# Attention's pipeline step -2 moves beside the patch stage, and the weights' transfers are issued in pieces

## The chip, the core and the metric

The kernel runs on one core of one Trainium2 chip. The metric is the time of one launch in microseconds (us), the median of several runs. The core has five engines with an instruction stream each: PE multiplies matrices, DVE and POOL work elementwise on the on-chip memory (SBUF), ACT does scaled copies and exponentials, and SP only issues transfers (DMAs). They meet through semaphores.

## The reference

64 images of 3 x 224 x 224 become 64 x 196 tokens of 192 numbers; two attention layers, an MLP and a mixture of four experts follow.

```python
x = patches of 16 x 16 x 3                           # one row of 768 for each of 64 * 196 tokens
x = layernorm(x, ln1_g, ln1_b) @ W + b
h = layernorm(x, ln2_g, ln2_b)                       # "tokens", 12544 x 192
h = h + attention(layernorm(h))                      # 12 heads of 16, over the 196 tokens of an image
n = layernorm(h)
x = n + attention(layernorm(n, g, b)); x = x + mlp(x)
h = h + x + (the two best of 4 experts(layernorm(x)), weighted)
```

## The kernel before

`vit_tower` (L2333 and after) runs two blocks. In the first, `attention_phase` builds the programs of the two attention layers and calls `tokenize_phase`, the patch stage; in the second, `ffn_phase` does the MLP and the experts. Names of tiles begin with `t_` in the patch stage, with `a_` in attention and with `f_` after it.

*The patch stage.* The images are read in 8 groups of 16 images and 7 rows of patches, into two row buffers (`rows`) that take turns. A group has 7 units of two patch columns each, so there are 56 units. `steps` (in `tokenize_phase`) is written out for s = -3 to 56, and in each step every engine does its part of up to four units, by `LAG`: "A" is unit s+3 (DVE: statistics of the rows), "B" is unit s+1 (ACT normalises to `xn`, PE turns it, ACT and DVE split it into a high half `xh` and a low half `xl`), "C" is unit s (PE: the product with the weights into `yp`, DVE: its statistics), "D" is unit s-1 (ACT: L1356 writes `t_yn`; POOL: L1292 and L1294 apply gain and offset; SP: L1263 stores it to `tokens`). POOL works out scale and shift for "A" and "C" in four small instructions (L1305 to L1311). There are four `t_yn` buffers, and ACT waits for the store of unit u-4 before it writes unit u. SP loads the next group's rows (L1234) in four quarters, in the steps of a group's first four units.

*What runs beside it.* After each of its steps every engine calls its own `beside_patches(s)` of attention, a list written by hand: which part of attention's preparation it does after step s. There the weights of both layers are loaded (`load_weights`, SP, after steps 4 and 5), turned by PE, scaled by ACT and split by DVE, and the first units of layer 0 are started.

*Attention.* A unit is two images, 392 tokens; a layer has 32 units, so there are 64. A unit goes through a pipeline: load ("W", 5 steps ahead), scale and norm on POOL ("X", 4 ahead), turning, high and low halves and two row products ("L", 3 ahead), the third row product, the stores to a scratch tensor `a_qk` and the first half of its stacks `qst` and `kst` ("P", 2 ahead), the other half, row maxima and values ("M", 1 ahead), scores, exponentials and weighted sums ("C"), and three steps behind that. `steps` (in `attention_phase`) runs s = -2 to 66, partly in loops. Step -2 holds "W" of unit 3, "X" of unit 2, "L" of unit 1 and "P" of unit 0; step -1 has the first maxima, step 0 the first exponentials. Each engine starts its part (`attend`) when it is through with the patch stage, after waits: PE for all of the patch stage's `t_yn` and for 12 settings (`set_s`), of which the six memsets of `stack_borders` on DVE are the last.

*Memory.* `qst`, `kst`, `vp` and `pt` are allocated after the patch stage's tiles are released, so they lie where these lay and can't be written before the patch stage is over.

## Time and profile before

| what | value |
|---|---|
| median of 3 runs | 3089.83 us (3086.55 to 3103.68) |
| the profiled execution | 3087.19 us |
| its span | 3085.5 us |
| PE, DVE, ACT, POOL busy | 89%, 75%, 61%, 55% |
| patch stage and weights | 0 to about 371 us |
| attention steps -2 and -1 | about 371 to 404 us |
| attention, two layers | about 405 to 1850 us |
| experts | about 1850 us to the end |

The profile is one execution, read on the core's own clock from 0. A row of a timeline says when an engine ran an instruction (or some of one kind after each other, "x2"), how long, and in brackets how long the engine had been idle before it and who released it. The granted clock is TensorE's: 1.00 is its full 2.4 GHz, 0.50 the lower level of 1.2 GHz, and what lies between is a stretch with both.

### The profile page before, as it was taken

The numbers are of one execution on the slowest core, as the hardware profiler recorded it, in microseconds if no ns is written. First come the engines' busy times: TensorE is split into PE (matmuls) and PEld (weight loads), VectorE is DVE, ScalarE is ACT, GpSimd is POOL, SyncE is SP. The second block draws the span as 40 slices with busy tenths as digits, with TensorE's granted clock in tenths as the row PEclk, the third lists the DMA queues.
The fourth block names the chain that finished last, engine by engine and source line by source line (L and its number), as shares of the span: only waits on it lengthen the run. The fifth ranks groups of instructions, "written<-read, shape, count | busy, mean of one in ns | idle before, by whom it ended". The sixth has DMA issues, their size and how long they took to land. (4 is left out here: it accounts for less than half of the span.)

```text
span 3085.5 us, 95504 instructions
## 1 busy us (share of the span) xinstructions
PE 2732.0 (89%) x31491; PEld 2124.6 (69%) x31491; DVE 2311.9 (75%) x5326; ACT 1878.1 (61%) x3798; POOL 1682.0 (55%) x1957
## 2 busy tenths in 40 slices
PE   5798788999899998989998967999986999999998
PEld 5688645555555555555555546899975888888887
DVE  5689678788878887877788735877765777777776
ACT  5577556667666666666666636777753444444443
POOL 3467635555455666667666432567674444444444
PEclk9899989999999999999999968999987999999999
DMA  6555256676766667676767635444433444444443
GB/s 159 161 157 166 58 121 155 145 164 149 157 142 152 165 163 167 161 173 160 175 159 174 143 76 136 147 147 147 143 126 91 68 67 65 68 67 65 69 66 47
DMA packets 515433, 395.07 MB, mean 128 GB/s; under 512 B 223136, under 2 KB 488386, under 8 KB 515138
## 3 DMA queue, kind: packets, MB, share of 16 engines
q1 hardware_dynamic: 431426, 310.47, 41.3%
q0 software_dynamic: 38496, 46.38, 8.5%
q10 hardware_dynamic: 45216, 34.34, 4.6%
q8 instruction: 179, 2.93, 0.4%
q14 instruction: 116, 0.95, 0.1%
HBM read 232.59 MB, written 155.42 MB: 126 GB/s over the span
## 5 line engine op out<-in xcount | busy, mean ns | idle before, releaser
L814 DVE TENSOR_REDUCE a_mx<-a_mxp 98x4 f32<-98x784 f32 x768 | 747.0, 973 | 268.6 <-PE a_mxp L1000 265.9
L603 ACT ACTIVATE a_pt<-a_st 98x784 f32<-98x784 f32 x768 | 634.6, 826 | 352.8 <-PE a_st L986 351.9
L1817 POOL DMA_INDIRECT out_dram<-f_yo,f_idg x202 | 330.9, 1638 | 415.6 <-DVE f_yo L2158 378.9
L500 POOL TENSOR_TENSOR a_cf<-a_ctxs,a_rec 128x1176 f32<-128x1176 f32 x64 | 171.6, 2681 | 448.1 <-DMA a_rec<-a_recip 448.1
L1895 ACT ACTIVATE f_hf<-f_bank,f_b1c 128x256 f32<-128x256 f32 x606 | 254.3, 473 | 236.0 <-PE f_bank L1128 236.0
L1015 PE MATMUL a_pv<-a_pt,a_vp 98*32 98x196 f32 x6144 | 358.7, 352 | 5.0 <-issue 4.1
L986 PE MATMUL a_st<-a_qst,a_kst 49*128 49x196 f16 x3072 | 266.7, 253 | 78.6 <-DMA a_qst<-a_mrow 53.5
L2320 PE MATMUL f_bank<-f_w2h,f_hh 128*128 x1212 | 298.9, 247 | 19.0 <-DVE f_hl L2142 18.7
L2321 PE MATMUL f_bank<-f_w2h,f_hl 128*128 x1212 | 298.2, 246 | 0.0
L2322 PE MATMUL f_bank<-f_w2l,f_hh 128*128 x1212 | 298.2, 246 | 0.0
L1000 PE MATMUL a_mxp<-a_kst,a_qst 48*128 48x196 f16 x3072 | 263.6, 250 | 28.8 <-DVE a_mx L814 21.5
L986 PEld LDWEIGHTS a_st<-a_qst,a_kst 49*128 49x128 f16 x3072 | 88.2, 95 | 280.2 <-ACT a_pt L603 131.0
L1015 PEld LDWEIGHTS a_pv<-a_pt,a_vp 98*32 98x32 f32 x6144 | 215.8, 151 | 72.9 <-issue 58.6
L1788 POOL DMA_INDIRECT f_listed<-f_xr,f_idx x196 | 209.6, 1069 | 76.1 <-issue 44.5
L1128 PE MATMUL f_bank<-f_el,f_w1h 128*128 128x256 f16 x1212 | 232.1, 273 | 0.0
L2142 DVE TENSOR_TENSOR f_hl<-f_hf,f_hh 128x512 f16<-128x512 f32 x303 | 209.9, 693 | 10.4
L1848 ACT ACTIVATE f_hh<-f_bank,f_b1c 128x256 f16<-128x256 f32 x294 | 141.0, 480 | 107.9 <-PE f_bank L1128 105.5
L1887 ACT ACTIVATE f_xf<-f_bank,f_bcol,f_gcol 128x256 f32<-128x256 f32 x202 | 103.2, 561 | 169.1 <-PE f_bank L2290 169.1
L1000 PEld LDWEIGHTS a_mxp<-a_kst,a_qst 48*128 48x128 f16 x3072 | 123.2, 96 | 78.8 <-DVE a_mx L814 62.7
L1128 PE MATMUL f_bank<-f_eh,f_w1h 128*128 128x256 f16 x606 | 165.6, 273 | 3.5 <-DVE f_el L2132 3.5
L1128 PE MATMUL t_yp<-t_wh,t_xh 128*112 128x192 f16 x672 | 168.2, 250 | 0.0
L1128 PE MATMUL t_yp<-t_wl,t_xh 128*112 128x192 f16 x672 | 167.6, 249 | 0.0
(314 smaller groups left out, 8269.9 us busy)
## 6 DMA issues: line engine op xcount, KB each, us to landing
a_rec<-a_recip SPq DMA_DIRECT2D x256, 147.0 KB, 4.9
t_rows<-in_x_dram SPq DMA_DIRECT2D x84, 392.0 KB, 5.7
a_qst<-a_qk SPq DMA_DIRECT2D x256, 110.2 KB, 3.2
a_kst<-a_qk SPq DMA_DIRECT2D x256, 110.2 KB, 4.0
f_xg<-f_listed SPq DMA_DIRECT2D x101, 264.0 KB, 2.8
a_qk<-a_qkh SPq DMA_DIRECT2D x128, 196.0 KB, 3.1
a_qk<-a_qkl SPq DMA_DIRECT2D x128, 98.0 KB, 3.4
a_qk<-a_qkh SPq DMA_DIRECT2D x128, 98.0 KB, 2.5
```

The lines of the kernel that those rows point to most:

```text
L603: act.activation(pt[k % PT][:].rearrange("p j a t -> p j (a t)"), st_ps[0:half_t, :, 0:unit_t], ACT.Exp, scale=sm_scale).then_inc(exp_s, 1)
L814: dve.tensor_reduce(mx[:, a, :, 2 * p:2 * p + 2].rearrange("p q j -> p j q"), mx_ps[0:half_t, :, 0:unit_t].rearrange("p j (q t) -> p j q t ...
L986: ins = pe.matmul(st_ps[:, j, kt * tok:(kt + 1) * tok], kst[b][part, p, a, at:at + 128], qst[b][part, p, a, 0:tok], start=True, stop=True)
L1000: ins = pe.matmul(mx_ps[:, j, qt * tok:(qt + 1) * tok], qst[b][part, p, a, at:at + 128], kst[b][part, p, a, 0:tok], start=True, stop=True)
L1015: ins = pe.matmul(pv_ps[32 * h4:32 * h4 + 32, 0:tok], vp[b][:, 2 * a + kt, :].rearrange("p (c h) -> p c h", h=heads)[:, :, h], pt[(first + ...
L1128: ins = pe.matmul(out, lhs, rhs, start=(i == 0), stop=(i == len(terms) - 1))
L1817: pool.indirect_dma_start(out, bass.IndirectOffsetOnAxis(ap=idg[i % 3][:, t:t + 1], axis=0), yo[i % 3][:, t, :], None, compute_op=ALU.add) ...
L1895: act.activation(hf[pair][:, c % 2, :], p1[q % 2][:, (c % 2) * T:(c % 2) * T + T], ACT.Gelu, bias=b1c[:, bass.ds(e, 1), c], scale=1.0 / WS ...
L2142: dve.tensor_tensor(hl[i % 2][:, cs, :], hf[pair][:], hh[i % 2][:, cs, :], ALU.subtract).then_inc(ehl_s, 1)
L2320: pe.matmul(o, hh[i % 2][:, j, ts], high, start=(j == 0), stop=False)
L2321: pe.matmul(o, hl[i % 2][:, j, ts], high, start=False, stop=False)
L2322: pe.matmul(o, hh[i % 2][:, j, ts], low, start=False, stop=False)
```

## The change

`load_weights` is cut into four functions with the same transfers, which SP issues after other steps of the patch stage: layer 0's after steps 3, 4 and 5, layer 1's after steps 10, 11, 12 and 17. The work of attention's step -2 goes into the `beside_patches` lists of all five engines, and what stood in these lists for the first units is put some steps earlier. `steps` of attention begins at -1. So that stacks can be filled while patches are worked on, `qst`, `kst`, `vp` and half of the `pt` buffers are allocated before everything else, and the first row buffer, `rows0`, is laid over them: it is read for the last time by the seventh group, the last but one. The memsets of `kst` move from DVE to POOL (after steps 50 and 55) with a semaphore of their own, `edge_s`, for which SP and PE wait; the wait for the last `t_yn` moves from PE's `attend` into the first `turn_maxima`. The lists of the diff are, in order, SP's, POOL's, ACT's, DVE's and PE's.

```diff
+        shared = -(-nc.sbuf_base // 32) * 32
+        qst = [sb(f"qst{i}", [128, pairs, 2, tok + PAD], F16) for i in range(2)]
+        kst = [sb(f"kst{i}", [128, pairs, 2, tok + PAD], F16) for i in range(2)]
+        vp = [sb(f"vp{i}", [half_t, 4, 32 * heads], F32) for i in range(2)]
+        pt = [sb(f"pt{i}", [half_t, 2, 2, tok], F32) for i in range(PT // 2)]
+        assert nc.sbuf_base - shared >= 4 * 3 * 16 * 224
...
-            at = -2
+            at = -1
...
-            def load_weights(layer):
+            def load_input_weights(layer):
...
+            def load_input_biases(layer):
...
+            def load_output_weights(layer):
...
+            def load_vectors(layer):
...
             def beside_patches(s):
+                if s == 3:
+                    load_input_weights(0)
+                    load_input_biases(0)
                 if s == 4:
-                    load_weights(0)
+                    load_output_weights(0)
                 if s == 5:
-                    load_weights(1)
-                if s == 38:
+                    load_vectors(0)
+                if s == 10:
+                    load_input_weights(1)
+                if s == 11:
+                    load_input_biases(1)
+                if s == 12:
+                    load_output_weights(1)
+                if s == 17:
+                    load_vectors(1)
+                if s == 34:
                     for done in patches["stored"]:
                         sp.wait_ge(done, 16 * 4)
                     load_rows(0, 0, 0)
-                if s == 41:
+                if s == 37:
                     load_rows(1, 1, 0)
-                if s == 48:
+                if s == 46:
                     load_rows(2, 0, 0)
+                if s == 51:
+                    store_parts(0, 0, 0)
+                    store_parts(0, 0, 1)
+                    store_parts(0, 0, 2)
+                if s == 52:
+                    store_parts(0, 0, 3)
+                if s == 53:
+                    sp.wait_ge(edge_s, 1)
+                    load_stacks(0, 0, 0, 0)
+                    load_stacks(0, 0, 0, 1)
+                if s == 54:
+                    load_rows(3, 1, 0)
...
-                sp.wait_ge(set_s, SET)
+                sp.wait_ge(edge_s, 2)
...
-                if s == 42:
+                if s == 39:
                     scale_tokens(0, 0, 0)
-                if s == 43:
+                if s == 40:
                     norm_tokens(0, 0, 0)
+                if s == 46:
+                    scale_tokens(1, 1, 0)
                 if s == 47:
-                    scale_tokens(1, 1, 0)
-                if s == 48:
                     norm_tokens(1, 1, 0)
+                if s == 50:
+                    pool.wait_ge(patches["read"], patches["reads"])
+                    pool.memset(kst[0][:], MROW).then_inc(edge_s, 1)
+                if s == 53:
+                    scale_tokens(2, 0, 0)
+                if s == 54:
+                    norm_tokens(2, 0, 0)
+                if s == 55:
+                    pool.memset(kst[1][:], MROW).then_inc(edge_s, 1)
...
-                if s == 45:
+                if s == 42:
                     high_part(0, 0, 0)
                     high_part(0, 0, 1)
+                if s == 46:
+                    high_rows(0, 0, 0, 0)
+                if s == 47:
+                    high_rows(0, 0, 1, 0)
                 if s == 49:
-                    high_rows(0, 0, 0, 0)
-                if s == 50:
-                    high_rows(0, 0, 1, 0)
+                    high_rows(0, 0, 2, 0)
+                if s == 52:
+                    high_part(1, 1, 0)
+                    high_part(1, 1, 1)
+                if s == 55:
+                    high_rows(1, 1, 0, 0)
+                if s == 56:
+                    high_rows(1, 1, 1, 0)
...
-            def stack_borders():
+            def borders(i):
                 dve.wait_ge(patches["read"], patches["reads"])
-                for i in range(2):
-                    dve.memset(kst[i][:], MROW).then_inc(set_s, 1)
-                    dve.memset(qst[i][:, :, :, tok:tok + PAD], 0.0).then_inc(set_s, 1)
-                    dve.memset(vp[i][:, :, 2 * dim - heads:2 * dim], 1.0).then_inc(set_s, 1)
+                dve.memset(qst[i][:, :, :, tok:tok + PAD], 0.0).then_inc(set_s, 1)
+                dve.memset(vp[i][:, :, 2 * dim - heads:2 * dim], 1.0).then_inc(set_s, 1)
...
-                if s == 40:
+                if s == 36:
                     statistics(0, 0, 0)
+                if s == 37:
                     statistics(0, 0, 2)
+                if s == 38:
+                    aggregate(0, 0)
                 if s == 41:
-                    aggregate(0, 0)
+                    statistics(1, 1, 0)
+                if s == 42:
+                    statistics(1, 1, 2)
+                if s == 43:
+                    low_part(0, 0, 0)
                 if s == 44:
-                    statistics(1, 1, 0)
+                    low_part(0, 0, 1)
                 if s == 45:
-                    low_part(0, 0, 0)
-                if s == 46:
-                    low_part(0, 0, 1)
-                    statistics(1, 1, 2)
                     aggregate(1, 0)
+                if s == 47:
+                    low_rows(0, 0, 0, 0)
+                if s == 48:
+                    low_rows(0, 0, 1, 0)
+                if s == 49:
+                    statistics(2, 0, 0)
                 if s == 50:
-                    low_rows(0, 0, 0, 0)
+                    low_rows(0, 0, 2, 0)
                 if s == 51:
-                    low_rows(0, 0, 1, 0)
+                    statistics(2, 0, 2)
                 if s == 52:
-                    statistics(2, 0, 0)
+                    aggregate(2, 0)
+                    borders(0)
+                if s == 53:
+                    low_part(1, 1, 0)
+                    low_part(1, 1, 1)
+                if s == 54:
+                    borders(1)
+                if s == 55:
+                    statistics(3, 1, 0)
+                if s == 56:
+                    low_rows(1, 1, 0, 0)
+                    low_rows(1, 1, 1, 0)
...
-                stack_borders()
...
-                if s == 44:
+                if s == 41:
                     pe.wait_ge(w_f[1], G_READY[1] + 4)
                     turn_rows(misc[BANK["T0"]], 0, 0)
                     turn_rows(misc[BANK["T1"]], 0, 1)
-                if s == 48:
+                if s == 45:
                     for layer in range(NL):
                         pe.wait_ge(w_ok[layer], 5)
-                    rows(take("QK0", -3), 0, 0, 0, 0)
-                if s == 49:
-                    rows(take("QK1", -3), 0, 0, 1, 0)
+                    pe.wait_ge(xl_s, 1)
+                    rows(misc[BANK["QK0"]], 0, 0, 0, 0)
+                if s == 46:
+                    pe.wait_ge(xl_s, 2)
+                    rows(misc[BANK["QK1"]], 0, 0, 1, 0)
+                if s == 48:
+                    pe.wait_ge(ql_s, 1)
+                    rows(misc[BANK["QK2"]], 0, 0, 2, 0)
+                if s == 51:
+                    pe.wait_ge(ql_s, 3)
+                    turn_rows(misc[BANK["T0"]], 1, 0)
+                    turn_rows(misc[BANK["T1"]], 1, 1)
+                if s == 54:
+                    pe.wait_ge(xl_s, 3)
+                    rows(misc[BANK["QK0"]], 1, 1, 0, 0)
+                if s == 55:
+                    pe.wait_ge(xl_s, 4)
+                    rows(misc[BANK["QK1"]], 1, 1, 1, 0)
...
+                if isinstance(u, int) and u == 0 and a == 0:
+                    pe.wait_ge(patches["normed"], patches["norms"])
...
-                pe.wait_ge(patches["normed"], patches["norms"])
                 pe.wait_ge(set_s, SET)
+                pe.wait_ge(edge_s, 2)
...
-        qst = [sb(f"qst{i}", [128, pairs, 2, tok + PAD], F16) for i in range(2)]
-        kst = [sb(f"kst{i}", [128, pairs, 2, tok + PAD], F16) for i in range(2)]
-        vp = [sb(f"vp{i}", [half_t, 4, 32 * heads], F32) for i in range(2)]
-
-        pt = [sb(f"pt{i}", [half_t, 2, 2, tok], F32) for i in range(PT)]
+        pt += [sb(f"pt{i}", [half_t, 2, 2, tok], F32) for i in range(PT // 2, PT)]
...
-        rows = [sb(f"rows{i}", [R, chans, line], F32) for i in range(2)]
+        rows = [nc.alloc_sbuf_tensor_at("t_rows0", [R, chans, line], F32, offset=told["rows0"]), sb("rows1", [R, chans, line], F32)]
...
-        told["read"], told["reads"] = xn_s, 2 * NU
+        told["read"], told["reads"] = xn_s, 2 * ((n_groups - 1) * UPG)
```

The first place is SP's queue around the weights (each row issues transfers; `t_rows` are image rows, which a `_50` behind the name doesn't change; `tokens<-t_yn` is a store of the patch stage). Before, the end of layer 1's 31 transfers, ahead of the third group's rows and a store:

```order
L289 DMA a_praw<-in_L_ffn_out_w_dram 96x12x16
L292 DMA a_pbias<-in_L_ffn_out_b_dram 96x1 x2
L295 DMA a_bv<-in_L_ffn_in_b_dram 98x192
L299 DMA a_gcol<-in_L_ffn_ln_g_dram 128x1
L301 DMA a_gcol<-in_L_ffn_ln_g_dram 64x1 x2
L299 DMA a_bcol<-in_L_ffn_ln_b_dram 128x1
L301 DMA a_bcol<-in_L_ffn_ln_b_dram 64x1 x2
L1234 DMA t_rows<-in_x_dram 112x1x896 [waits t_st_s,t_xn_s]
L1234 DMA t_rows<-in_x_dram 112x1x896 x2
L1263 DMA tokens<-t_yn 16x7x384 [waits t_aff]
L1234 DMA t_rows<-in_x_dram 112x1x896 x3
```

Now, at the same rows of the third group:

```order
L314 DMA a_bv<-in_L_attn_b_qkv_dram 98x192
L1324 DMA t_rows_50<-in_x_dram 112x1x896 [waits t_st_s,t_xn_s]
L1324 DMA t_rows_50<-in_x_dram 112x1x896 x2
L1353 DMA tokens<-t_yn 16x7x384 [waits t_aff]
L1324 DMA t_rows_50<-in_x_dram 112x1x896 x3
L1353 DMA tokens<-t_yn 16x7x384 [waits t_aff]
L1324 DMA t_rows_50<-in_x_dram 112x1x896 x3
L1353 DMA tokens<-t_yn 16x7x384 [waits t_aff]
L1324 DMA t_rows_50<-in_x_dram 112x1x896 x3
L1353 DMA tokens<-t_yn 16x7x384 [waits t_aff] x2
L272 DMA a_wraw<-in_L_ffn_in_w_dram 96x1x192
```

Layer 1's transfers stand behind the group's rows now, and stores stand between their four pieces.

The second place is POOL's stream at the end of the patch stage in the new kernel (numbers are buffer numbers; `t_shift1` ends the part of step 55, `t_yn3` is the last unit):

```order
L1395 TENSOR_TENSOR t_rstd1<-t_mv1,t_eps 112x2 [waits t_yn_s,t_mv2_s]
L1397 TENSOR_TENSOR t_rstd1<-t_rstd1,t_minus_half 112x2 [waits t_norm_s]
L1399 TENSOR_TENSOR t_shift1<-t_mv1,t_rstd1 112x2 [waits t_norm_s]
L1401 TENSOR_TENSOR t_shift1<-t_shift1,t_minus_one 112x2 [waits t_norm_s]
L498 MEMSET a_kst1 128x2712
L1382 TENSOR_TENSOR t_yn3<-t_yn3,t_g2 112x384 [waits t_yn_s]
L1384 TENSOR_TENSOR t_yn3<-t_yn3,t_b2 112x384 [waits t_aff]
L1199 UNCONDITIONAL_BRANCH
```

The memset is new here; before, `t_yn3` followed `t_shift1` at once.

The third place is PE's stream where the patch stage ends (the branch) and attention begins. Before:

```order
L1128 MATMUL t_yp1<-t_brow_parts,t_first_two 112x192
L1121 UNCONDITIONAL_BRANCH
L1045 MATMUL a_misc0<-a_ident,a_xn 128x98 [waits a_ql_s,a_xn_s,a_set_s,t_yn_s]
L1045 MATMUL a_misc0<-a_ident,a_xn 128x98 x3
L1047 MATMUL a_misc1<-a_ident,a_xn 128x98 [waits a_xn_s,a_ql_s]
L1047 MATMUL a_misc1<-a_ident,a_xn 128x98 x3
L1128 MATMUL a_misc0<-a_xh0,a_wh0 128x392 [waits a_xl_s]
```

Now:

```order
L1218 MATMUL t_yp1<-t_brow_parts,t_first_two 112x192
L1218 MATMUL a_misc1<-a_xh1,a_wh0 128x392 [waits a_xl_s]
L1218 MATMUL a_misc1<-a_xh1,a_wl0 128x392
L1218 MATMUL a_misc1<-a_xl1,a_wh0 128x392 x2
L1218 MATMUL a_misc1<-a_xl1,a_wl0 128x392
L1211 UNCONDITIONAL_BRANCH
L1218 MATMUL a_misc0<-a_wh0,a_xh0 128x192 [waits a_ql_s,a_edge_s,a_set_s]
```

The turned rows (`a_ident`) and the row products (128x392) stand ahead of the branch now, and attention begins with a value product (128x192), which waits for `a_edge_s` and no longer for `t_yn_s`.

## Rows read from the trace of the kernel before

**Rows 1.** The page: busy time of each engine (share of the span) x instructions.
```profile
PE 2732.0 (89%) x31491; PEld 2124.6 (69%) x31491; DVE 2311.9 (75%) x5326; ACT 1878.1 (61%) x3798; POOL 1682.0 (55%) x1957
```

**Rows 2.** Stretches: start:end, length, busy time of engines, granted clock, DMA share, GB/s.
```profile
80.00:92.00 12.00, 11.21 (x121) 10.40 (x122) 11.11 (x40) 9.60 (x14) 8.75 (x16) 1.00 0.26 43
...
92.00:104.00 12.00, 2.64 (x32) 2.46 (x30) 2.74 (x11) 0.63 (x2) 0.28 (x2) 0.69 0.63 168
```

**Rows 3.** Timeline of ACT: start us, duration, engine, line, instruction, [idle before <-releaser].
```profile
87.41 0.91 ACT L1356 ACTIVATE t_yn<-t_yp,t_shift,t_rstd 112x192 f32<-112x192 f32 x2 [0.56 <-POOL t_shift L1311]
...
103.37 0.91 ACT L1356 ACTIVATE t_yn<-t_yp,t_shift,t_rstd 112x192 f32<-112x192 f32 x2 [11.62 <-DMA tokens<-t_yn]
...
124.12 0.91 ACT L1356 ACTIVATE t_yn<-t_yp,t_shift,t_rstd 112x192 f32<-112x192 f32 x2 [0.43 <-POOL t_shift L1311]
```

**Rows 4.** Timeline of SP's queue (each row is the issuing of DMAs).
```profile
74.63 0.59 SPq L1263 DMA_DIRECT2D tokens<-t_yn  x1
...
75.26 0.77 SPq L264 DMA_DIRECT2D a_wraw<-in_L_ffn_in_w_dram  x1
...
94.72 1.10 SPq L301 DMA_DIRECT2D a_bcol<-in_L_ffn_ln_b_dram  x2
...
95.95 1.92 SPq L1234 DMA_DIRECT2D t_rows<-in_x_dram  x3
...
97.91 0.62 SPq L1263 DMA_DIRECT2D tokens<-t_yn  x1
...
104.29 1.88 SPq L1234 DMA_DIRECT2D t_rows<-in_x_dram  x3
```

**Rows 5.** Timeline of DVE, the wait for the third group of image rows.
```profile
117.24 1.94 DVE L1389 BATCH_NORM_STATS2 t_stats<-t_rows 112x6 f32<-112x384 f32 x4 [22.05 <-DMA t_rows<-in_x_dram]
```

**Rows 6.** Timeline of ACT and of POOL: one undisturbed patch step.
```profile
280.29 0.91 ACT L1356 ACTIVATE t_yn<-t_yp,t_shift,t_rstd 112x192 f32<-112x192 f32 x2 [0.57 <-POOL t_shift L1311]
...
285.27 0.91 ACT L1356 ACTIVATE t_yn<-t_yp,t_shift,t_rstd 112x192 f32<-112x192 f32 x2 [0.63 <-POOL t_shift L1311]
...
281.28 1.00 POOL L1292 TENSOR_TENSOR t_yn<-t_yn,t_g 112x384 f32<-112x384 f32 x1 [1.03 <-ACT t_yn L1356]
...
285.04 0.20 POOL L1311 TENSOR_TENSOR t_shift<-t_shift,t_minus_one 112x4 f32<-112x4 f32 x1
```

**Rows 7.** Timeline of ACT around scale_tokens(0) and norm_tokens(0) on POOL.
```profile
295.89 0.91 ACT L1356 ACTIVATE t_yn<-t_yp,t_shift,t_rstd 112x192 f32<-112x192 f32 x2 [0.59 <-POOL t_shift L1311]
...
301.54 0.91 ACT L1356 ACTIVATE t_yn<-t_yp,t_shift,t_rstd 112x192 f32<-112x192 f32 x2 [1.29 <-POOL t_shift L1311]
...
308.30 0.91 ACT L1356 ACTIVATE t_yn<-t_yp,t_shift,t_rstd 112x192 f32<-112x192 f32 x2 [1.33 <-POOL t_shift L1311]
```

**Rows 8.** Timeline of DVE: one attention instruction beside the patches.
```profile
338.99 0.59 DVE L844 SCALAR_TENSOR_TENSOR a_qkl<-a_misc,a_bq,a_qkh 128x392 f16<-128x392 f32 x1
```

**Rows 9.** Timeline of POOL and DVE: memsets, and POOL's last patch row.
```profile
51.94 0.56 POOL L415 MEMSET a_pbias<- 96x256 f32 x2
...
366.89 0.20 POOL L1311 TENSOR_TENSOR t_shift<-t_shift,t_minus_one 112x2 f32<-112x2 f32 x1
...
364.57 2.32 DVE L683 MEMSET a_kst<- 128x2712 f16 x1 [0.51 <-issue]
```

**Rows 10.** The end of the patches: a stretch, and PE's timeline.
```profile
362.00:371.00 9.00, 1.68 (x18) 1.51 (x15) 6.50 (x13) 1.83 (x4) 5.62 (x10) 0.74 0.13 39
...
370.32 0.88 PE L1045 MATMUL a_misc<-a_ident,a_xn 98*128 98x98 f32 x4 [7.32 <-issue]
...
380.15 0.26 PE L1128 MATMUL a_misc<-a_wh,a_xh 128*128 128x192 f16 x1 [0.57 <-DVE a_qkl L844]
...
384.64 0.34 PE L1000 MATMUL a_mxp<-a_kst,a_qst 48*128 48x196 f16 x4 [2.67 <-DMA a_kst<-a_qk]
```

**Rows 11.** DVE's first maximum; the tile view of `a_pt`: durations, first and last start.
```profile
385.02 0.98 DVE L814 TENSOR_REDUCE a_mx<-a_mxp 98x4 f32<-98x784 f32 x1 [4.16 <-PE a_mxp L1000]
...
L603 ACT ACTIVATE a_pt<-a_st x768: 808/824/864, 404.7 to 1822.8; 98x784 f32<-98x784 f32 x192
```

More of the change, by code:

```diff
@@ L151, in attention_phase @@
         set_s = sem("set_s")
+        edge_s = sem("edge_s")
         p_ok = [sem(f"p_ok{i}") for i in range(NL)]
@@ L245, in attention_phase @@
         g_rows, r_rows, o_rows = [[layer[i].rearrange("(t p) d -> p t d", p=half_t) for layer in layers] for i in range(3)]
-        W_READY, G_READY, W_LOADS, SET = [], [], [], 12
+        W_READY, G_READY, W_LOADS, SET = [], [], [], 10
         for *_, head_major, affine in layers:
@@ L267, in load_weights @@
                     sp.dma_start(wraw[layer][:, 4:6, dim:256], w_rows[:, 4:6, 128:dim]).then_inc(w_in[layer], 16)
+                else:
+                    sp.dma_start(wraw[layer][:, :, 0:dim], w_rows).then_inc(w_in[layer], 16)
+                    sp.dma_start(wraw[layer][:, :, dim:256], w_rows[:, :, 128:dim]).then_inc(w_in[layer], 16)
+            def load_input_biases(layer):
+                _, _, _, w_qkv, b_qkv, w_proj, b_proj, head_major, affine = layers[layer]
+                if head_major:
                     b_rows = b_qkv[0:2 * dim].rearrange("(w h d) -> w d h", w=2, h=heads)
@@ L293, in load_weights @@
                                      b_proj[e * rows_q:(e + 1) * rows_q].rearrange("(p o) -> p o", o=1)).then_inc(w_in[layer], 16)
+            def load_vectors(layer):
+                _, _, _, w_qkv, b_qkv, w_proj, b_proj, head_major, affine = layers[layer]
                 bv_row = b_qkv[2 * dim:3 * dim]
@@ L1069, in attend @@
             def attend():
-                pe.wait_ge(patches["normed"], patches["norms"])
                 pe.wait_ge(set_s, SET)
+                pe.wait_ge(edge_s, 2)
                 steps(step, pe)
             return beside_patches, attend
-        patches = {}
+        patches = {"rows0": shared}
         sync_early, sync_attend = sync_program(nc.sync, patches)
```

3 lines of the change are left out of this document (1 added, 2 removed).

## Prediction

> **What bounds the kernel now.** I read the page, then the busy time by stretches, then the timelines of each engine over the first 410 us. The reader is to see two things. First, no engine limits the whole: PE is busy 89% of the span and DVE 75% [rows 1], and the change touches only the first 405 us, the patch stage and the way from it into attention. Second, this part has two losses.
>
> The patch stage is a chain of 60 steps with a period of its own. In an undisturbed step ACT's normalisation of `t_yn` starts at 280.29 and the next at 285.27, so 4.98 us; most lie between 4.9 and 5.1. The chain is: ACT writes `t_yn`, POOL starts on it 0.99 us later (281.28), does two products and sums of 1.00 us, then the four small instructions of `t_rstd`/`t_shift`, the last of which starts at 285.04, and that releases ACT's next one [rows 6]. POOL stands idle for 1.03 us in it. So an instruction put into POOL's step costs what it takes less 1.03 us. A check: `scale_tokens(0)` stretches one period to 5.65 (+0.7) and `norm_tokens(0)` the next to 6.76 (+1.8) [rows 7].
>
> The first loss: after the `t_yn` at 87.41 the next comes at 103.37 and waits 11.62 us for a transfer `tokens<-t_yn`, and three periods later we are at 124.12 [rows 3]. SP's queue says why: it stores `t_yn` at 74.63, issues the 31 transfers of layer 1's weights from 75.26 to 95.82 (0.66 us each), then three of the image rows at 95.95, and only at 97.91 the next store [rows 4]. There are four `t_yn` buffers, so ACT may not write the tenth unit before the sixth is stored. The same blockade delays the image rows of the third group: their last quarter is issued at 104.29, and DVE waits 22.05 us for them until 117.24 [rows 5].
>
> The second loss: PE's last patch product ends at 363.0, and it then waits 7.32 us for POOL's, DVE's and ACT's last patch work and DVE's border memsets, computes the whole of the pipeline step s = -2 (unit 1's turned rows, three row products), and gets the first maximum to DVE at 385.02, after another wait of 2.67 us for stacks. The first exponential runs at 404.7 [rows 10, 11]. In the stretch 362 to 371 PE does 1.68 us of work [rows 10].
>
> **The change, part by part.**
>
> *Weights in pieces (front).* The same 41 transfers are issued, no byte less. Layer 0's ten go at steps 3, 4 and 5 (3, 6 and 1), layer 1's at 10, 11, 12 and 17 (10, 8, 6 and 7). At 0.66 us the worst pieces take 6.6, 5.3 and 4.0 us beside stores of 0.6 and periods of 5: SP falls behind by 2 to 4 us from step 10 to 13 and catches up by 14. A store may be four periods late (20 us) before ACT feels it, and the fourth group's rows are due only at step 18, so both waits should go. The third group's rows are issued at steps 6 to 9, and the last by about 88; DVE needs them at about 95.2, 7 us later. Before, they were issued within 10 us of each other and the last took 11 us to land (106.2 to 117.2 [rows 4, 5]). Spread over 15 us I expect them in time, with up to 2 us of stall left as the bound. The sum: from 87.41 to 124.12 are 36.7 us; three periods of 4.98 [rows 6] are 14.9, and for layer 0's weight work in steps 10 and 11 I add 0.7, an estimate: what `scale_tokens` costs [rows 7]. That is 15.6. **Saved 21.1**; bounds 17 (rows late, and SP's delay felt) and 23 (PE's clock, 0.69 in the stall [rows 2], recovers sooner). What is late next: nothing on SP, but the POOL-ACT chain, which sets the period again.
>
> The Trainium skill ("DMA: Bandwidth & Descriptors", section "Issuing engines are not separate DMA queues") says that the time a sequencer takes to initiate a DMA is usually small relative to the DMA itself. Here it is not: while SP issued layer 1's weights, the 16 DMA engines were busy 0.26 of the time [rows 2]. By that rule the stall would be the transfers' own and would stay, and the result would be 3079 in place of 3058.
>
> *Attention's step -2 moves beside the patches (seam).* It adds nothing in total: unit 2's scale and norm (POOL), unit 0's third row product, unit 1's turned rows and two row products (PE), their ACT and DVE halves, the stores to `a_qk` and unit 0's first stacks (SP, 12 transfers, in steps 51 to 53, where no image rows are issued). It is paid where it lands in the POOL-ACT chain:
> - POOL: `scale_tokens(2)` +0.7, `norm_tokens(2)` +1.8 [rows 7].
> - POOL: the memset of `a_kst0`, before on DVE with 2.32 us for 2712 elements. On POOL no row shows this size. From below: two memsets of 256 elements take 0.56 [rows 9], so 0.28 each, at least; a packed form could be half of DVE's, 1.1. From above: a POOL product of 384 elements takes 1.00 [rows 6], 2.6 ns each, so 7.1. I take 2.3, since the small memset's 1.1 ns per element with its fixed part in it is near DVE's 0.86 and far from 2.6. In the chain: +1.3 (bounds 0 and +6.1).
> - DVE: it is nearly full (11.11 of 12.00 us [rows 2]); a third row product's low part at 0.59 [rows 8], two more statistics at about that, an aggregate and the two small borders: +1.0 (0 to 2). From step 53 on DVE has no image statistics any more, and the work there is free.
> - ACT and PE: copies of unit 1 at steps 52, 55 and 56, +0.3; PE's products fit into its waits.
>
> So POOL's last `t_shift`, which ended at 367.1 [rows 9], ends 5.1 later; then the memset of `a_kst1` runs, and PE may enter attention only behind it (`edge_s`): 367.1 + 5.1 + 2.3 = 374.5, in the time of before. PE then does two value products (1.8 us: from 380.15 to 382.0, where its next wait of 2.67 us begins) and its first turned score, and DVE's first maximum, 0.4 behind it, starts at 376.9 in place of 385.02 [rows 10, 11]. **Saved 8.1.** The half of unit 0's stacks that is not yet loaded is issued after the last store (367.1, and 3.1 for the last `t_yn`, as in [rows 6]; + 5.1 + 1.3 = 376.6), lands by about 383 and is needed six maxima later, at about 386, both estimates: just covered. If not, the price is 1 to 3 us. The bounds of the whole part: with memsets of 7.1 us each costs 4.8 more, which leaves 8.1 - 9.6 = -1.5; with cheap ones and no cost on DVE, 13.
>
> *The rest.* Stacks, values and half of the `pt` buffers lie elsewhere in SBUF; from the first exponential on, every engine has the same instructions in the same order. I cost that at nothing. The sum: 3087.2 (this execution; its span 3085.5 and 1.7 around it; the median of the runs is 3089.8, 2.6 above) - 21.1 - 8.1 = **3058**.
>
> **The rivals.**
> 1. *Only the front gains.* The memsets on POOL cost what POOL's products cost, or the second half of the stacks comes late, and the seam brings only 3 us or loses 1.5: 3063 to 3068. For it: POOL is in the chain of every patch step, and no row shows a large memset on it. Against: the two small ones [rows 9]. 16 in 100.
> 2. *The front stall stays*, because the transfers themselves and not their issue made it (the skill's rule), or moves to steps 10 to 14: 3079, no measurable change. For it: DMA share 0.63 during the stall. Against: 0.26 before it, and that 0.63 began when the image rows were at last issued [rows 2, 4]. 6 in 100; that neither part gains, 3087, 3 in 100.
> 3. *Slower: the attention loop runs slower in its new place.* Its 64 units of 12 exponentials take from 404.7 to 1822.8 [rows 11], 22 us each; stacks and `pt` lie at other addresses, and the queues enter the loop in another phase to each other. The 29 us saved are gone at 0.46 us per unit, and at 0.75 us the kernel takes 3106. No row shows such a dependence, and none excludes it. 4 in 100.
> Both gains, as forecast: 71 in 100.
>
> **How the numbers follow.** The forecast's own range is 3047 to 3066. Rival 1 reaches 3068, with the 2.6 us between this execution and the median, and the bound of late rows, to 3073. So 3046 to 3073 holds the time 8 times in 10. A measurement of this kernel can tell about 0.5% (15 us, so 3074) from no change: its three runs lie 17 us apart. Faster: 0.71 + 0.16 = 0.87. Same: 0.09. Slower: 0.04.
>
> **What would show it.** Front right: the tenth `t_yn` follows the ninth after 5 us, without a wait for `tokens<-t_yn`, and DVE's wait for `t_rows` is under 2 us; PE's clock is 1.00 from 80 to 125. Seam right: a POOL memset of `a_kst` of 2 to 3 us at two places, first maximum about 29 us earlier than 385, first exponential about 29 us earlier than 404.7, and from there to the end 2682 us as before (3087.2 - 404.7). It is wrong if the memset takes over 5 us, if PE waits for `a_kst<-a_qk` in the middle of the maxima, if the periods of steps 10 to 14 exceed 6 us, or if the attention units take longer.

## The result and the profile after

The changed kernel takes 3074.43 us (median of 10 runs, 3052.88 to 3085.66), the kernel before 3095.43 us (median of 10, 3086.55 to 3111.17). The ratio is 0.9937, with a 95% interval from 0.991 to 0.9963: faster, by 0.6%, and less than forecast. The forecast of 3058 is 16 us too low, and the measured median lies 1.4 us above the range. The profiled execution took 3069.66 us, with a span of 3067.9.

The first 380 us of the trace did what was forecast. The stretches that answer to [rows 2], of the changed kernel (columns as there):

```profile
80.00:92.00 12.00, 11.09 (x116) 10.07 (x117) 10.81 (x42) 9.86 (x15) 8.75 (x16) 1.00 1.04 278
92.00:104.00 12.00, 11.12 (x126) 10.51 (x125) 11.01 (x36) 10.42 (x19) 8.27 (x15) 1.00 0.43 113
```

The second stretch had PE at 2.64 us of 12 and a clock of 0.69; now PE is as busy as in the first, at full clock. ACT's timeline, for [rows 3], shows the tenth unit 5 us behind the ninth and no wait for a store:

```profile
88.27 0.92 ACT L1446 ACTIVATE t_yn<-t_yp,t_shift,t_rstd 112x192 f32<-112x192 f32 x2 [0.56 <-POOL t_shift L1401]
93.27 0.91 ACT L1446 ACTIVATE t_yn<-t_yp,t_shift,t_rstd 112x192 f32<-112x192 f32 x2 [0.65 <-POOL t_shift L1401]
98.19 0.91 ACT L1446 ACTIVATE t_yn<-t_yp,t_shift,t_rstd 112x192 f32<-112x192 f32 x2 [0.57 <-POOL t_shift L1401]
103.17 0.91 ACT L1446 ACTIVATE t_yn<-t_yp,t_shift,t_rstd 112x192 f32<-112x192 f32 x2
```

SP's queue in the same place, for [rows 4]: the stores stand between the pieces, and the fourth group's rows follow at 114.64.

```profile
103.35 0.44 SPq L275 DMA_DIRECT2D a_wraw<-in_L_ffn_in_w_dram  x1
103.83 0.62 SPq L1353 DMA_DIRECT2D tokens<-t_yn  x1
104.49 4.99 SPq L294 DMA_DIRECT2D a_bq<-in_L_ffn_in_b_dram  x8
109.93 0.64 SPq L1353 DMA_DIRECT2D tokens<-t_yn  x1
...
114.64 1.88 SPq L1324 DMA_DIRECT2D t_rows<-in_x_dram  x3
```

The wait of DVE for rows that [rows 5] shows is gone for the third group. One of 1.07 us is left, for the fourth:

```profile
136.37 1.94 DVE L1479 BATCH_NORM_STATS2 t_stats<-t_rows 112x6 f32<-112x384 f32 x4 [1.07 <-DMA t_rows<-in_x_dram]
```

The end of the patch stage, for [rows 9 to 11]: timelines of POOL, PE, DVE and ACT. The two memsets take 2.36 us each, PE enters attention 0.1 behind the second, the first maximum is at 356.12 and the first exponential at 375.68. The last row is the last exponential.

```profile
321.77 2.36 POOL L492 MEMSET a_kst<- 128x2712 f16 x1
...
349.81 2.36 POOL L498 MEMSET a_kst<- 128x2712 f16 x1
...
352.27 0.32 PE L1218 MATMUL a_misc<-a_wh,a_xh 128*128 128x192 f16 x1 [7.66 <-POOL a_kst L498]
...
356.12 0.98 DVE L892 TENSOR_REDUCE a_mx<-a_mxp 98x4 f32<-98x784 f32 x1 [4.15 <-PE a_mxp L1092]
...
375.68 0.82 ACT L663 ACTIVATE a_pt<-a_st 98x784 f32<-98x784 f32 x1 [1.29 <-PE a_st L1078]
...
1805.39 0.82 ACT L663 ACTIVATE a_pt<-a_st 98x784 f32<-98x784 f32 x1 [0.45 <-PE a_st L1078]
```

Both came 28.9 and 29.0 us earlier than before, where 29 was forecast. But of these 29 us only 17.5 are left at the end of the profiled execution (3087.19 to 3069.66). From the first to the last exponential it took 1429.71 us, and before 1418.16. After the last exponential both took the same, 1262.5 and 1262.7. So the question is what happened in the attention loop, where both kernels have the same instructions in the same order. The view of busy time over the loop shows nearly the same work and a slightly lower granted clock, first the changed kernel, then the kernel before:

```profile
375.68:1805.39 1429.71, 1289.80 (x16858) 806.14 (x16860) 1120.90 (x1915) 964.18 (x1834) 823.37 (x1012) 0.97 0.66 154
```

```profile
404.66:1822.82 1418.16, 1282.99 (x16858) 801.91 (x16860) 1114.56 (x1915) 962.41 (x1835) 824.04 (x1012) 0.98 0.67 155
```

Going through the loop unit by unit (from the first exponential of one to that of the next, 63 stretches), the 54 units of before that ran wholly at full clock took 21.99 us on average, and the 51 of the changed kernel 21.89. The difference is in the others: 9 before, 12 now. Three theories follow. **Theory C** (clock): the clock falls by chance, in some units of each execution, whatever the kernel. **Theory A** (addresses): the new place of stacks and `pt` makes the loop slower. **Theory P** (phase): the engines enter the loop in another phase to each other, in which the clock falls more often. A is the forecast's third rival; P is the second half of it.

### The profile page after: what moved, and what is told of

The parts are those of the page before. It is cut to its first block and busy times, and to the rows that moved or that the text cites. A ratio compares the mean times of both kernels' runs of the same rounds, so it can differ in the third digit from the quotient of the medians.

```text
span 3067.9 us, 95505 instructions
## 1 busy us (share of the span) xinstructions
PE 2735.1 (89%) x31491; PEld 2122.8 (69%) x31491; DVE 2311.6 (75%) x5324; ACT 1878.7 (61%) x3798; POOL 1686.3 (55%) x1959
## 5 line engine op out<-in xcount | busy, mean ns | idle before, releaser
L1218 PE MATMUL t_yp<-t_wh,t_xl 128*112 128x192 f16 x672 | 166.7, 248 | 0.0
```

What stands on the lines that cost most here:

```text
L1218: ins = pe.matmul(out, lhs, rhs, start=(i == 0), stop=(i == len(terms) - 1))
```

## The experiments

All 14 profiled executions, the first two and twelve of experiments, in one table. "Loop" is first to last exponential. "Low" is the loop's time at the low clock: for each stretch of 2 us the part by which the granted clock is under 1.00, on the scale on which 0.50 counts as the whole stretch. "Tail" is the span less the last exponential.

| kernel | first exponential | loop | low | loop - low/2 | tail |
|---|---|---|---|---|---|
| before | 404.66 | 1418.2 | 62 | 1387 | 1262.7 |
| before, e12 | 408.37 | 1434.1 | 98 | 1385 | 1261.8 |
| changed | 375.68 | 1429.7 | 79 | 1390 | 1262.5 |
| changed, e4 | 376.47 | 1432.9 | 82 | 1392 | 1274.9 |
| changed, e8 | 375.59 | 1432.9 | 89 | 1388 | 1261.3 |
| changed, e11 | 374.55 | 1418.4 | 68 | 1384 | 1262.3 |
| front only, e1 | 385.86 | 1417.1 | 53 | 1391 | 1276.6 |
| seam only, e2 | 397.14 | 1419.0 | 72 | 1383 | 1272.5 |
| addresses only, e3 | 402.99 | 1419.9 | 59 | 1390 | 1263.5 |
| memsets on DVE, e5 | 372.69 | 1414.1 | 58 | 1385 | 1278.9 |
| memsets on DVE, e10 | 371.42 | 1431.3 | 91 | 1386 | 1276.4 |
| weights whole at step 10, e7 | 382.79 | 1425.4 | 67 | 1392 | 1259.8 |
| fillers at two places, e6 | 376.56 | 1430.0 | 29 | 1416 | 1264.7 |
| filler at one place, e9 | 376.05 | 1426.4 | 66 | 1393 | 1275.2 |

**e1, the front alone.** The kernel before, with this and the four functions:

```diff
-                if s == 4:
-                    load_weights(0)
-                if s == 5:
-                    load_weights(1)
+                if s == 3:
+                    load_input_weights(0)
+                    load_input_biases(0)
+                if s == 4:
+                    load_output_weights(0)
+                if s == 5:
+                    load_vectors(0)
+                if s == 10:
+                    load_input_weights(1)
+                if s == 11:
+                    load_input_biases(1)
+                if s == 12:
+                    load_output_weights(1)
+                if s == 17:
+                    load_vectors(1)
```

> The kernel before, with the weights' transfers in pieces as in the changed kernel (after steps 3, 4, 5, 10, 11, 12, 17) and nothing else. In the changed kernel's profile the first 29 us were saved as forecast, but from the first exponential to the last it took 1429.7 us in place of 1418.2, and 12 of its units held a stretch at the low granted clock in place of 9. Theory C (clock): the loop's length differs from execution to execution with the number of such stretches, about 3.5 us each, whatever the kernel. Then the first exponential comes 21 us before 404.66, at 383.6, the loop takes 1418 to 1430 and its length follows the count, and the time is 21 us (0.7%) below before: ratio 0.993. Theory A (addresses: stacks and pt lie elsewhere, each unit 0.18 us slower) and theory P (the loop is entered in another phase by the seam) say here: loop 1418 as before, ratio 0.993.

Measured: 3072.91 us (6 runs) against 3100.48 (25 runs of before), ratio 0.9906 (0.9879 to 0.9933), so 27.6 us where 21 were expected; 21 lies at the edge of the interval. The ninth and tenth `t_yn` are 4.99 apart:

```profile
86.70 0.91 ACT L1378 ACTIVATE t_yn<-t_yp,t_shift,t_rstd 112x192 f32<-112x192 f32 x2 [0.56 <-POOL t_shift L1333]
91.69 0.91 ACT L1378 ACTIVATE t_yn<-t_yp,t_shift,t_rstd 112x192 f32<-112x192 f32 x2 [0.64 <-POOL t_shift L1333]
```

An execution's first `t_yn` starts anywhere from 44.9 to 48.0, so the patch stage is compared from there. By unit 14 the front has saved 21.9 us, and by the last unit 18.6, since the image rows' arrival stretches other steps by one or two us from one execution to the next. The first exponential came at 385.86 and not at 383.6. The loop is 1417.1: no theory is hurt.

**e2, the seam alone.** The changed kernel, with all four functions of layer 0 called at `s == 4` and all of layer 1 at `s == 5`.

> The changed kernel, with the weights' transfers whole again after steps 4 and 5. All theories: the stall of the front is back (the tenth t_yn some 15 us behind the ninth), and the first exponential comes 8 us before 404.66, at 396.7. Theory C: the loop is 1418 to 1430 by the count of low stretches, ratio 0.9975. Theory A and theory P: the loop is 1430, 11.5 longer than before, so the kernel is 3.5 us slower than before, ratio 1.001.

Measured: 3096.76 us (12 runs), ratio 0.9982 (0.9957 to 1.0008). The stall is back at its old size:

```profile
86.41 0.91 ACT L1441 ACTIVATE t_yn<-t_yp,t_shift,t_rstd 112x192 f32<-112x192 f32 x2 [0.56 <-POOL t_shift L1396]
102.43 0.91 ACT L1441 ACTIVATE t_yn<-t_yp,t_shift,t_rstd 112x192 f32<-112x192 f32 x2 [11.67 <-DMA tokens<-t_yn]
```

The first exponential is at 397.14, 7.5 earlier than 404.66. From the first `t_yn` to the last are 324.7 us where the first profile of before has 320.1, so the work in the patch steps costs 4.5; from the last `t_yn` to the first exponential are 26.5 us and before 37.5, so 11.1 are gained there. The 4.5 is not firm: the second profile of before (e12) has 323.5, and against it the cost is 1.2. With the front in place the seam can be read too: from the first `t_yn` to the first exponential e1 has 339.6 us and the four profiles of the changed kernel 327.8 to 328.6, so 11.0 to 11.8 are gained, with only 0.5 lost in the patch steps. The loop is 1419.0, not the 1430 of A and P in their plain form.

**e3, the addresses alone.** The kernel before with the allocation of the changed one:

```diff
+        shared = -(-nc.sbuf_base // 32) * 32
+        qst = [sb(f"qst{i}", [128, pairs, 2, tok + PAD], F16) for i in range(2)]
...
+        pt = [sb(f"pt{i}", [half_t, 2, 2, tok], F32) for i in range(PT // 2)]
...
-        patches = {}
+        patches = {"rows0": shared}
```

> The kernel before with all work where it was, but qst, kst, vp and half of pt allocated first and the first row buffer laid over them, so that every tile lies where it lies in the changed kernel. Theory A: the loop takes 1430 us, each unit at full clock 0.18 us longer than the 21.9 to 22.0 of before, and the kernel is 11.5 us slower, ratio 1.004. Theory C and theory P: no change, ratio 1.000, loop 1418 to 1430 by the count of low stretches.

Measured: 3097.17 us (12 runs), ratio 0.9988 (0.9966 to 1.001), loop 1419.9, units at full clock 22.03 us. Theory A, which asked for a ratio of 1.004 and a loop of 1430, falls.

**e4 and e8, the changed kernel again.**

> The changed kernel unchanged, beside the three others on the same chip, for a second profile and a narrower interval. Theory C: first exponential again at 375.7 within 1 us, the loop of another length than 1429.7, by about 3.5 us for each stretch at the low clock more or less, and over many executions the mean saving is 29 us, ratio 0.9906. Theory A and theory P: loop 1430 again, ratio 0.9945.

> The changed kernel a third time, for its attention loop alone. It took 1429.7 and 1432.9 us, the five others 1417 to 1420. Theory C (chance): it lies anywhere from 1415 to 1435, by the time at the low clock (length less half of that time was 1383 to 1392 in all six). Theory P (both parts together bring the loop into a phase with more falls): 1428 to 1434 again, with about 80 us at the low clock.

Measured: e4 3078.34 us (8 runs, 3054.74 to 3091.97), ratio 0.99 (0.9865 to 0.9936); its loop took 1432.9. e8 took 3071.51 in its one run, loop 1432.9. Three loops of the changed kernel were now longer than all six others without fillers, and theory P looked right. It had to be tested with more executions, and they undid it (e10 to e12).

**e5 and e10, the memsets on DVE.** The changed kernel, with POOL's two memsets of `kst` taken out and put into `borders`:

```diff
-                if s == 50:
-                    pool.wait_ge(patches["read"], patches["reads"])
-                    pool.memset(kst[0][:], MROW).then_inc(edge_s, 1)
...
-                if s == 55:
-                    pool.memset(kst[1][:], MROW).then_inc(edge_s, 1)
...
                 dve.wait_ge(patches["read"], patches["reads"])
+                dve.memset(kst[i][:], MROW).then_inc(edge_s, 1)
```

> The changed kernel with the two memsets of kst back on DVE, each in front of the two small borders of its step (52 and 54), where DVE has no image statistics any more. In the changed kernel's profile PE waits 7.66 us for the second memset on POOL (it ends at 352.17), and the first stretched its step by 1.3. If POOL's memsets are what is left of the seam: the last t_yn comes 1.3 us earlier than 349.92; the first maximum is then set by DVE's two low parts of unit 1 behind ACT's halves, at 350.7 in place of 356.1, and the first exponential at 370.3 in place of 375.7; the whole is 5 us faster than the changed kernel, ratio to before 0.990. Rival: DVE is as full as POOL there, the two memsets of 2.3 us push its work for units 53 to 55 behind, or the second half of the stacks is late, and the first exponential stays within 1 us of 375.7.

> The version with the memsets on DVE again. Its first profile had the shortest loop of all, 1414.1 us with 57 us at the low clock, while it enters the loop only 3 us earlier than the changed kernel, whose three loops took 1429.7, 1432.9 and 1432.9. Theory P (the moment at which the engines enter the loop sets how often the clock falls): the loop takes 1414 again, within 4 us. Theory C (chance): anywhere from 1414 to 1435. Time against before: ratio 0.990 again.

Measured: 3065.71 us (6 runs), ratio 0.99 (0.9866 to 0.9934), and 3065.09 us (6 runs), ratio 0.9872 (0.9822 to 0.9921). From the last `t_yn` to the first exponential it took 24.7 us both times, against 25.8 to 26.5 with POOL's memsets. From the first `t_yn` on, e5 gains 1.6 to 2.4 us, not the 5 expected. PE's timeline says why: PE now waits for DVE's low part of unit 1 before it goes on to the first maxima, and that stands behind ACT's half, which stands behind the last `t_yn`.

```profile
345.57 0.32 PE L1214 MATMUL a_misc<-a_wh,a_xh 128*128 128x192 f16 x1 [2.93 <-DVE a_qkl L918]
350.13 0.35 PE L1214 MATMUL a_misc<-a_wh,a_xh 128*128 128x192 f16 x1 [2.80 <-DVE a_qkl L918]
```

The loops took 1414.1 and 1431.3 us, with 58 and 91 us at the low clock. The same kernel, entered at the same moment (372.69 and 371.42), has the shortest loop of the series and one of the longest. Theory P said 1414 again. The version is faster than before; that it beats the changed kernel by more than these 2 us is not shown (the mean of its 12 runs is 3067.8, that of 20 of the changed kernel 3072.6, each uncertain by 5 to 6).

**e6, fillers where PE waits.** A closer look at one fall of the clock in the changed kernel, busy time in stretches of 2 us and two rows of PE's timeline:

```profile
532.00:534.00 2.00, 1.59 (x28) 0.83 (x28) 1.87 (x2) 1.69 (x5) 2.00 (x1) 1.00 0.80 227
534.00:536.00 2.00, 0.98 (x7) 0.67 (x8) 1.92 (x5) 1.54 (x4) 1.92 (x2) 0.75 0.45 108
536.00:538.00 2.00, 2.00 (x17) 1.31 (x15) 1.04 (x2) 1.13 (x3) 0.55 (x1) 0.50 0.68 193
538.00:540.00 2.00, 2.00 (x22) 0.90 (x23) 0.98 (x2) 0.38 (x2) 0.00 (x0) 0.50 0.38 120
540.00:542.00 2.00, 2.00 (x19) 1.68 (x16) 1.27 (x6) 1.04 (x2) 0.04 (x1) 0.55 0.04 9
542.00:544.00 2.00, 2.00 (x32) 1.32 (x31) 1.04 (x2) 1.00 (x2) 1.69 (x5) 1.00 0.00 0
```

```profile
530.54 0.34 PE L1078 MATMUL a_st<-a_qst,a_kst 49*128 49x196 f16 x4 [0.99 <-DMA a_qst<-a_mrow]
...
535.02 0.51 PE L1092 MATMUL a_mxp<-a_kst,a_qst 48*128 48x196 f16 x4 [1.43 <-DVE a_mx L892]
```

PE has waited 0.99 us for a transfer and 1.43 us for DVE's maximum; then its clock is at the lower level for 6 to 7 us, in which PE is busy all the time, so that the unit takes 24.87 us in place of 21.9. The other falls look alike, though the low stretch is 3.4 us in some, 6.8 in others and 10.2 in one. In the middle of the loop (from 20 us behind the first exponential to 1740) of before, of the changed kernel, of e5 and of e8 there are 34, and ahead of each PE had waited 0.7 us or more in the 8 us before, ahead of 20 of them twice. But such a wait alone does not bring a fall: PE has 222 of them in these four stretches, and behind 169 no fall came within 8 us. The edit writes products that nobody reads into these waits:

```diff
+            def keep_busy(bank, n):
+                for _ in range(n):
+                    pe.matmul(bank[:, 0:196], wh[0][:, 0, 0:128], wh[0][:, 0, 0:196], start=True, stop=True)
...
+                        if k == 0 and "C" in kinds:
+                            keep_busy(take("V0", s), 6)
                         values(take(f"V{n}", s), s + 1, (par + 1) % 2, n, kinds["M"])
...
                     if "C" in kinds:
                         scores(s, par, k)
+                    if k == 2 and "C" in kinds and "L" in kinds:
+                        keep_busy(take("T0", s), 8)
```

> The changed kernel with work added on PE that computes nothing used: in every attention step 6 products of 128 x 196 ahead of the values, and 8 ahead of the second turned scores of the step, just where PE waits 1.0 and 1.4 us in the profile and where the granted clock falls afterwards. Theory C (the clock falls behind these idle stretches, and each fall costs about 3.5 us): with the idle stretches filled the falls go, the loop's time at the low clock drops from 80 us to under 30, and the loop takes 1395 us in place of 1430: 30 us faster than the changed kernel, ratio 0.982, with less spread between executions. Rival B (PE's work is the bound in the loop, and the clock matters little): 14 products of 0.1 us in each of 64 units make it up to 90 us slower, at least 20. Theory A and theory P (loop longer by address or phase) say nothing against either, but then the loop stays 10 us over what the count of falls gives.

Measured: 3076.05 us (11 runs), ratio 0.9925 (0.9902 to 0.9949). Here is the middle of the loop, with the fillers, and about the same stretch of the changed kernel:

```profile
396.56:1780.00 1383.44, 1303.30 (x17262) 841.60 (x17261) 1089.67 (x1878) 945.44 (x1783) 807.17 (x997) 1.00 0.67 156
```

```profile
395.68:1780.00 1384.32, 1252.00 (x16391) 785.71 (x16393) 1096.71 (x1875) 933.83 (x1782) 807.00 (x997) 0.98 0.67 156
```

The 1.00 is rounded. No fall is left from 396.56 to 1740; three of 3.4 us come after that, at 1749, 1763 and 1773, where the second place has no filler any more (its last ones run at 1725). The first of them:

```profile
1748.00:1754.00 6.00, 5.71 (x66) 4.09 (x70) 2.59 (x4) 3.07 (x7) 2.60 (x2) 0.72 0.31 83
```

So the falls do follow from PE's waits. But nothing is won, neither the 30 us that theory C expected nor the loss of 20 of rival B: units at full clock take 22.41 us in place of 21.9, 0.5 times 64 units, which is as much as the falls had cost. At the second place the filler itself waits for ACT's copy of the values:

```profile
714.28 0.85 PE L1075 MATMUL a_misc<-a_wh 128*128 128x196 f16 x8 [0.33 <-ACT a_vp L692]
```

**e9, filler at one place.** The version of e5, with the 6 products ahead of the values alone.

> The version with the memsets on DVE, and of the added PE work only the 6 products ahead of the values (nothing ahead of the turned scores, where they had to wait 0.33 us for ACT's copy of the values). With both places filled no fall of the clock was left in the loop, but its units at full clock took 22.41 us in place of 21.9, so 30 us were paid for 30 us. Theory C: six products of 0.08 us fit into the wait of 1.0 us there; the units stay at 21.9 to 22.1, the time at the low clock goes from 57 to 89 us down to 30 to 50, and the loop takes 1400 to 1412: 3050 to 3062 us, ratio 0.984. Rival: the first wait is not what the fall needs, the low time stays over 55 us, and the loop is 1415 to 1435.

Measured: 3072.37 us (6 runs), ratio 0.9896 (0.9852 to 0.994), low 66 us, loop 1426.4, units at full clock 22.11. The rival holds: filling the first wait is not enough, and falls still came behind waits of 0.5 to 1.6 us for DVE's maximum. A filler at the second place that waits for nothing was not tried.

**e7, layer 1's weights whole, but after step 10.** The changed kernel with all four functions of layer 0 at `s == 4` and of layer 1 at `s == 10`.

> The changed kernel, with layer 0's ten transfers together after step 4 and layer 1's 31 together after step 10, behind the third group's rows, so the same issue time of 20.6 us in one piece but at a place where no rows are due. If the late rows were the greater part of the stall and ACT may run four units ahead of the stores: the t_yn of units 9 to 18 lose under 3 us in all against the changed kernel (u14 at 119.5). Rival, by the stores alone: ACT waits again for a store, 5 to 12 us, with u18 at 148 to 155 in place of 143.3, and pieces are what counts and not the place.

Measured, one run: 3069.66 us. Against the changed kernel, both from their ninth `t_yn`, unit 14 is 1.2 us late, unit 18 is 5.2, and the last unit 9.4. No `t_yn` waits for a store. What is late is the fourth group's rows, issued behind the weights; DVE's timeline:

```profile
138.52 1.94 DVE L1474 BATCH_NORM_STATS2 t_stats<-t_rows 112x6 f32<-112x384 f32 x4 [4.12 <-DMA t_rows<-in_x_dram]
```

So neither expectation holds in full. Place alone gives most of the 21.9 us back by unit 14, the pieces are worth another 5 at unit 18, and why the last 4 are lost later is not settled by one execution.

**e11 and e12, both kernels once more.**

> The changed kernel a fourth time. Theory P: the loop takes 1429 to 1433 us for the fourth time, with 79 to 89 us at the low clock. Theory C: anywhere from 1414 to 1435.

> The kernel before a second time. Both theories: first exponential 357.7 us behind the first t_yn. Theory P: loop 1418 within 3 us, as in its first profile. Theory C: anywhere from 1414 to 1435.

Measured: the changed kernel 3056.97 us with a loop of 1418.4; before 3105.93 us with a loop of 1434.1. Together with e10, that refutes theory P as stated: neither the kernel nor the moment of entry fixes the loop's length. A small shift of the mean is not excluded, since the seven loops with both parts and without fillers average 1426.4 us and the five others 1421.7, 4.7 apart and uncertain by 8. Here are the two loops, e11 first; they have the clocks of the first pair, exchanged:

```profile
374.55:1792.95 1418.40, 1285.88 (x16860) 803.67 (x16860) 1117.93 (x1915) 961.61 (x1835) 822.52 (x1012) 0.98 0.66 155
```

```profile
408.37:1842.43 1434.06, 1298.31 (x16858) 810.81 (x16860) 1123.50 (x1915) 962.59 (x1835) 822.99 (x1013) 0.97 0.66 154
```

## Why the prediction was right in its steps and wrong in its number

**The front: right.** Forecast 21.1 us saved by unit 11, measured 20.95 in the profile [rows 3], and 21.9 by unit 14 in e1 counted from the first `t_yn`. DVE's wait of 22.05 us went, the clock stayed at 1.00 from 80 to 104, and the periods of steps 10 to 14 were 4.9 to 5.8. The rival that the transfers themselves made the stall is refuted by e2 (all of it back with the same bytes) and by the changed kernel, whose DMA share from 80 to 92 is 1.04 while the patch stage runs on undisturbed. The Trainium skill ("DMA: Bandwidth & Descriptors", section "Issuing engines are not separate DMA queues") calls a sequencer's time to initiate a DMA usually small relative to the DMA. For one transfer the trace agrees: the store issued at 74.63 before takes 0.59 us to issue and has landed 2.6 us after that time. What the prediction set against that sentence, a DMA share of 0.26, is no such comparison. The stall came from the sum: 31 issues of 0.66 us in one piece held image rows and stores back.

**The seam: right in its mechanism, its size known only to a few us.** The memset: 2.3 forecast, 2.36 measured. The cost in the patch steps: 5.1 forecast; 4.5 in e2 against the first profile of before, 1.2 against the second, 0.5 in the changed kernel against e1. The step from the second memset's end to the first maximum: 2.4 forecast, 3.95 measured (352.17 to 356.12). The forecast took the value products at full clock; behind PE's wait of 7.66 us the granted clock is 0.50 from 352 to 356, and the 20 products that took 1.8 us before (from 380.15, at 1.00) take 3.4. In all, 8.1 forecast for the first exponential; counted from the first `t_yn`, e2 has 6.5 against the first profile of before and 10.1 against the second, and the changed kernel 11.0 to 11.8 against e1. In the launch times the seam does not show: e2's interval holds 1, and the means of e1 (3074.1) and of the changed kernel (3072.6) are 1.5 us apart. The second half of unit 0's stacks was in time, as forecast: no maximum waits for `a_kst<-a_qk`.

**Both together.** First maximum and first exponential 29 us earlier: 28.9 and 29.0 in the first profile; 28.2 to 30.1 over four profiles of the changed kernel against the first of before, and 3.7 more against its second.

**The step that failed is the base of the sum:** "The sum: 3087.2 (this execution; its span 3085.5 and 1.7 around it; the median of the runs is 3089.8, 2.6 above)". That execution is no typical one. Of 62 executions of before, 4 took 3087.19 us or less; their median is 3100.0 us and the standard deviation 9.4. It had both a short loop (1418 of 1418 to 1434) and a short tail (1263 of 1260 to 1279). The forecast then asked for "2682 us as before" after the first exponential, the luck of one execution taken for a property of the kernel; the four of the changed kernel had 2694, 2709, 2696 and 2682 us there. And the range gave this base 2.6 us, on the strength of three runs that lay 17 us apart. With 29.2 taken from 3100.0 the forecast would have been 3070.8. The base is not all of the miss: from the first comparison's own median of before, 3095.4, the forecast would have been 3066.2, and the other 8.2 us are within the spread of ten runs, whose means there are 23.2 us apart, uncertain by 8. The range's lower end, 3046, has no sum either: the best bounds of both parts, 23 and 13, give 3051. The 20 executions of the changed kernel have a mean of 3072.6, the 62 of before 3100.8: 28.2 us apart, uncertain by 5.5; they are pooled over several sets of runs on more than one chip, so the figure is rough. The interval of the first comparison, 0.991 to 0.9963, just leaves the forecast saving (0.9906) out; that of e4 holds it.

**The third rival** (the loop slower in its new place) seemed to have come true in the first profile, 11.5 us or 0.18 us per unit. It had not: e3 refutes the addresses, and e10 to e12 refute a phase that fixes the loop's length. What remains is the clock, which varies from one execution of a kernel to the next: in 13 of the 14 executions (all but the fillers') the loop less half its time at the low clock is 1383 to 1393 us, while the loop itself spreads from 1414 to 1434. What decides in which units PE's waits come so that the clock falls is open.

## What to carry to other kernels

A queue that carries both bulk setup and just-in-time work needs its order checked for the second: count the issues ahead of each transfer that somebody waits for, times the time of one issue, and put the bulk where nothing is due (e7: that alone is most of it), in pieces shorter than the slack of what is queued behind. A stage that overlaps another is worth what the end of its chain gains less what its insertions cost on the engine that sets the period (in e2 11.1 less 4.5 us); both can be estimated before the change. And a saving is added to the median of many runs, never to one profiled execution; when one profile shows a stage of unchanged instructions slower, profile both kernels again before looking for a reason, since three equal results (1429.7, 1432.9, 1432.9) were still chance.

## What the runs showed of the hardware that was not expected

One kernel's executions spread by 46 us (3084.05 to 3129.63 over 62 of before), and two causes are visible. In the attention loop the granted clock falls to its lower level for 3.4 or 6.8 us, seldom longer, behind waits of PE of 0.7 to 2.2 us (the 34 falls read for e6), in 20 of the 34 behind two of them about 4 to 5 us apart. A fall costs about half its length, and a loop without fillers has 50 to 100 us of low clock. And the tail after attention has two levels that have nothing to do with the clock (about 110 to 120 us of low clock in each of the 14): 1260 to 1265 us in 8 executions, 1272 to 1279 in 6. What goes with it is the landing of the experts' scattered rows. Waits of DVE in the tail, for the changed kernel (tail 1262.5) and for e10 (1276.4); the columns are total, times and longest:

```profile
DVE f_mine L2238 <- DMA out_dram<-f_yo,f_idg: 9.5, 34, 0.4
```

```profile
DVE f_mine L2234 <- DMA out_dram<-f_yo,f_idg: 23.3, 43, 1.2
```

The 8 short tails have 9 to 18 us of this wait with a longest of 0.4 to 0.9, the 6 long ones 20 to 26 with a longest of 1.1 to 1.3. Both levels occur for the changed kernel, and why one execution gets the one or the other is open.
